# A state-space block: u by one Silu pass of ScalarE in place of tanh, copy and a VectorE multiply; step projection and skip products moved

## What is computed

```
xz = in_proj_w @ xn                       # 512 rows: x (256) and z (256)
for each direction (the second on reversed tokens):
    u = silu(causal_conv(x, conv_w) + conv_b)          # 256 x 512, four taps
    x_dbl = xproj_w @ u                                # 8 + 16 + 16 rows: steps, B, C
    delta = softplus(dtproj_w @ x_dbl[:8] + dt_bias)   # 256 x 512
    h[l] = exp(delta * A) * h[l-1] + delta * B * u     # 256 channels x 16 states
    y = (h * C).sum(states) + D * u
    out += y * silu(z)
result = x + out_proj_w @ out + quantised_linear(hadamard(xn))
```

## Time and profile before

| | |
|---|---|
| median of 3 runs | 977.38 us (975.98 to 980.18) |
| profiled execution | 976.08 us, span 974.0 us |
| TensorE busy | 765.9 us, 79% (3873 matmuls) |
| VectorE busy | 800.2 us, 82% |
| ScalarE busy | 782.1 us, 80% |
| GpSimd busy | 750.2 us, 77% |
| mean granted TensorE clock | 0.864 of full speed |
| DMA | 72.53 MB, mean 74 GB/s |

### The profile page before, as it was taken

How to read it: one execution, slowest core, us unless ns; L and a number is a source line. 1 busy time by engine, 2 the same in 40 slices (tenths; PEclk the granted TensorE clock), 3 DMA queues, 4 the chain that set the end, 5 groups by cost and what they waited for, 6 DMA issues and landing times.

```text
span 974.0 us, 13835 instructions
## 1 busy us (share of the span) xinstructions
PE 765.9 (79%) x3873; PEld 384.4 (39%) x3873; DVE 800.2 (82%) x838; ACT 782.1 (80%) x1454; POOL 750.2 (77%) x454
## 2 busy tenths in 40 slices
PE   3486977689786977979689697878978697797994
PEld 1233443343433435334353344434443343433452
DVE  2278988898788878888888887889878887897995
ACT  2599995899878987789967998589986898878970
POOL 2159887788768977789787887878886798777994
PEclk9788988889787988979889797988978798897797
DMA  3424225070620607024070512507052070702400
GB/s 91 113 66 118 48 79 107 4 163 4 141 55 30 135 3 172 24 70 91 30 166 3 126 38 70 124 3 162 3 126 68 10 154 3 172 14 68 95 7 27
DMA packets 51433, 72.53 MB, mean 74 GB/s; under 512 B 6704, under 2 KB 19920, under 8 KB 51408
## 3 DMA queue, kind: packets, MB, share of 16 engines
q1 hardware_dynamic: 50976, 71.97, 31.6%
q10 hardware_dynamic: 432, 0.26, 0.1%
HBM read 60.68 MB, written 11.53 MB: 74 GB/s over the span
## 4 chain that ended last, share of the span: by engine, by line
POOL 29%; issue 27%; PE 18%; ACT 15%; DVE 8%; DMA 2%; POOLq 1%; SPq 0%; DVEq 0%; ACTq 0%
POOL hst L678 22%; PE pb L792 5%; DVE hst L569 5%; ACT da L416 4%; POOL dbx_t L688 4%; PE b_ps L879 4%; ACT dbx_t L405 2%; PE y L894 2%; PE b_ps L864 1%; PE y L891 1%; POOL t_log L694 1%; ACT xn L308 1%; PE pb L856 1%; DVE b_ps L557 1%; PE pb L811 1%
## 5 line engine op out<-in xcount | busy, mean ns | idle before, releaser
L678 POOL TENSOR_TENSOR hst<-hst,c_rep 128x1024 f32<-128x1024 f32 x256 | 600.6, 2365 | 170.8 <-DVE hst L569 170.1
L569 DVE TENSOR_TENSOR_SCAN hst<-da,b_ps 128x512 f32<-128x512 f32 x512 | 586.3, 1202 | 43.1 <-ACT da L416 21.4
L879 PE MATMUL b_ps<-ident,dbx_t 128*128 128x128 f32 x1536 | 246.6, 301 | 158.3 <-DVE hst L569 157.4
L416 ACT ACTIVATE da<-rep,neg_a 128x511 f32<-128x511 f32 x512 | 336.2, 710 | 5.8 <-DVE hst L569 3.8
L879 PEld LDWEIGHTS b_ps<-ident,dbx_t 128*128 128x128 f32 x1536 | 181.0, 151 | 281.2 <-DVE hst L569 255.7
L405 ACT ACTIVATE dbx_t<-du_t,b_t 128x256 f32<-128x256 f32 x576 | 247.0, 496 | 2.5 <-PE b_ps L879 1.7
L894 PE MATMUL y<-hst,sum_sel 128*32 128x512 f32 x1024 | 148.9, 657 | 3.0 <-POOL hst L678 3.0
L792 PE MATMUL pb<-xnt,conv_wt 128*128 128x512 f32 x256 | 121.0, 617 | 0.8 <-ACT xnt L316 0.8
L688 POOL TENSOR_TENSOR dbx_t<-du_t,b_t 128x1024 f32<-128x1024 f32 x48 | 91.3, 1903 | 2.7 <-ACT du_t L388 2.7
L864 PE MATMUL b_ps<-t_log,spread_sel 32*128 32x512 f32 x256 | 73.4, 679 | 14.3 <-POOL t_log L740 9.8
L557 DVE TENSOR_TENSOR b_ps<-b_ps,b_rep 128x1024 f32<-128x1024 f32 x64 | 78.0, 1219 | 5.4 <-PE b_ps L864 5.4
(11 more groups left out here) (111 smaller groups left out, 588.5 us busy)
## 6 DMA issues: line engine op xcount, KB each, us to landing
rep<-d_scr SPq DMA_DIRECT2D x128, 256.0 KB, 9.1
c_rep<-bc_scr SPq DMA_DIRECT2D x64, 256.0 KB, 4.8
d_scr<-t_pos SPq DMA_DIRECT2D x15, 512.0 KB, 3.0
b_rep<-bc_scr SPq DMA_DIRECT2D x64, 64.0 KB, 2.2
x_ln<-x SPq DMA_DIRECT2D x8, 256.0 KB, 3.3
x_res<-x SPq DMA_DIRECT2D x8, 256.0 KB, 2.8
out<-x_res SPq DMA_DIRECT2D x8, 256.0 KB, 7.1
conv_wt<-conv_w SPq DMA_DIRECT2D x2, 512.0 KB, 5.8
```

The lines of the kernel that those rows point to most:

```text
L416: nc.scalar.activation(da[s % 2][:, j, 1:L], rep[d][h][:, j, 1:L], ACT.Exp, scale=neg_a[:, d, h, j, q:q + 1]).then_inc(decay_done, 1)
L569: nc.vector.tensor_tensor_scan(hst[s % RING][:, j, :], da[s % 2][:, j, :], b_ps[:, j, :], 0.0, ALU.mult, ALU.add).then_inc(scan_done, 1)
L678: nc.gpsimd.tensor_tensor(hst[s % RING][:, two, :], hst[s % RING][:, two, :], c_rep[d][:, q:q + 1, :].broadcast_to([P, 2, L]), ALU.mult).t ...
L879: ins = tr(b_ps[:, j, P * c:P * (c + 1)], dbx_t[(NX * d + q - 1) % 2][:, c, NJ * h + j, :, :].rearrange("p r e -> p (r e)"), ident[:, :])
```

## The change

u becomes one ScalarE activation with function Silu, reading the convolution's bank with the bias and writing u. Both halves follow each other at the end of slot 0, and VectorE has no u operation left. `half_bias` goes with it. keep_bt moves ahead of slot 2's second pair of decays. The projection weight is there once, x_dbl once (64 partitions), and two weight loads (four DMAs) fewer are issued. On TensorE `steps` for h = 1 moves to right behind `b_transposed`, between the two halves of slot 2's inputs; the skip products move from the sums to slot 3, between the two halves of slot 4's inputs (`SKIP_AT` is 3). Some waits change to match.

```diff
-        xproj = [sb(f"xproj{d}", [P, NH, 2, XC]) for d in range(2)]
+        xproj = [sb(f"xproj{d}", [P, NH, XC]) for d in range(2)]
...
-                for h in range(NH):
-                    sp.dma_start(xproj[d][:, :, h, 0:DR + 2 * NS], xproj_t[d]).then_inc(w_loaded, DMA)
-                    sp.dma_start(dtw[d][XC * h:XC * h + DR, :], dt_t[d]).then_inc(w_loaded, DMA)
+                sp.dma_start(xproj[d][:, :, 0:DR + 2 * NS], xproj_t[d]).then_inc(w_loaded, DMA)
+                sp.dma_start(dtw[d][0:DR, :], dt_t[d]).then_inc(w_loaded, DMA)
...
-            def u_sigmoid(d, V, h):
+            def make_u(d, V, h):
                 act.wait_ge(conv_filled, 2 * V + h + 1)
-                wait(act, delta_ready, V)
-                nc.scalar.activation(t_exp[:, h, :], pb[:, 1 - h, :], ACT.Tanh, bias=half_bias[:, d, h:h + 1], scale=0.5).then_inc(u_step, 1)
-                act.wait_ge(u_step, 2 * V + h + 1)
-                nc.scalar.activation(t_exp[:, h, :], t_exp[:, h, :], ACT.Copy, bias=0.5, scale=0.5).then_inc(u_sig, 1)
+                if h == 0:
+                    wait(act, sum_done, SLOTS * (V - 2) + SKIP_AT)
+                    wait(act, du_ready, V - 1)
+                nc.scalar.activation(u[d][:, h, :], pb[:, 1 - h, :], ACT.Silu, bias=col[:, d, 0, h:h + 1]).then_inc(u_ready, 1)
 
             def keep_xdbl(d, V):
...
-                nc.scalar.activation(xdbl[d][:, :], pb[:, 1, :], ACT.Copy).then_inc(xdbl_ready, 1)
+                nc.scalar.activation(xdbl[d][0:XC, :], pb[0:XC, 1, :], ACT.Copy).then_inc(xdbl_ready, 1)
...
             def softplus_in(d, V):
-                wait(act, u_ready, 2 * V + 2)
+                wait(act, delta_ready, V)
...
-                        if nxt:
-                            u_sigmoid(e, V, 1)
                     if s == 2:
                         if nxt:
                             keep_xdbl(e, V)
                         if d == 0 and not first(b):
                             keep_xqt(b - 1)
                         inputs_t(d, U, 2, 2)
+                        if nxt:
+                            keep_bt(e, V)
...
                     if s == 0:
                         inputs_t(d, U, 1, 2)
                         if nxt:
-                            u_sigmoid(e, V, 0)
+                            make_u(e, V, 0)
+                            make_u(e, V, 1)
...
                         if nxt:
-                            keep_bt(e, V)
                             softplus_in(e, V)
...
-            def make_u(d, V, h):
-                dve.wait_ge(u_sig, 2 * V + h + 1)
-                wait(dve, sum_done, SLOTS * (V - 2) + SKIP_AT)
-                nc.vector.scalar_tensor_tensor(u[d][:, h, :], pb[:, 1 - h, :], col[:, d, 0, h:h + 1], t_exp[:, h, :], ALU.add, ALU.mult).then_inc(u_ready, 1)
...
-                    ins = mm(pb[:, 1, :], xproj[d][:, h, :, :].rearrange("p r c -> p (r c)"), u[d][:, h, :], start=h == 0, stop=h == NH - 1)
+                    ins = mm(pb[0:XC, 1, :], xproj[d][:, h, :], u[d][:, h, :], start=h == 0, stop=h == NH - 1)
...
-                mm(pb[:, h, :], dtw[d][XC * h:XC * (h + 1), P * h:P * (h + 1)], xdbl[d][XC * h:XC * (h + 1), :], start=True, stop=True).then_inc(dt_filled, 1)
+                mm(pb[:, h, :], dtw[d][0:XC, P * h:P * (h + 1)], xdbl[d][0:XC, :], start=True, stop=True).then_inc(dt_filled, 1)
...
+            def skip_products(b, d):
+                step = slice(None, None, -1 if d else 1)
+                pe.wait_ge(u_ready, 2 * (2 * b + d) + 2)
+                for h in range(NH):
+                    mm(y[:, h, :], skip[:, d, h, :], u[d][:, h, step], start=False, stop=False, skip_group_check=True)
+
             def sum_states(b, d, s):
...
-                if s == SKIP_AT - 1:
-                    pe.wait_ge(u_ready, 2 * (2 * b + d) + 2)
-                    for n in range(NH):
-                        mm(y[:, n, :], skip[:, d, n, :], u[d][:, n, step], start=False, stop=False, skip_group_check=True)
...
                             b_transposed(e, V, u_ready, 2 * V + 2)
+                        steps(e, 1, xdbl_ready, V + 1)
+                    if s == SKIP_AT:
+                        skip_products(b, d)
...
                     if s == 1 and nxt:
-                        steps(e, 1, xdbl_ready, V + 1)
                         steps(e, 0, bt_ready, V + 1)
```

More of the change, by code:

```diff
@@ L50, in build @@
         col = sb("col", [P, 2, 3, NH])
-        half_bias = sb("half_bias", [P, 2, NH])
-        xproj = [sb(f"xproj{d}", [P, NH, 2, XC]) for d in range(2)]
+        xproj = [sb(f"xproj{d}", [P, NH, XC]) for d in range(2)]
         dtw = [sb(f"dtw{d}", [P, DI]) for d in range(2)]
@@ L137, in build @@
         conv_filled = sem("conv_filled")
-        u_step = sem("u_step")
-        u_sig = sem("u_sig")
         u_ready = sem("u_ready")
@@ L282, in _ @@
             sp.wait_ge(out_stored, DMA * NB)
-        W_LOADS = 7 + 8
+        W_LOADS = 7 + 4
         WIN = hst[0][:, 0, 0:DI]
@@ L354, in first_softplus @@
             def first_softplus():
-                act.wait_ge(u_ready, 2)
                 act.wait_ge(dt_filled, 1)
@@ L423, in _ @@
             nc.scalar.activation(neg_a[:, :, :, :, :], neg_a[:, :, :, :, :], ACT.Exp).then_inc(a_exp, 1)
-            act.wait_ge(weights_ready, 3)
-            u_sigmoid(0, 0, 0)
-            u_sigmoid(0, 0, 1)
+            make_u(0, 0, 0)
+            make_u(0, 0, 1)
             keep_xdbl(0, 0)
@@ L588, in _ @@
             dve.wait_ge(w_loaded, DMA * W_LOADS)
-            nc.vector.tensor_scalar(half_bias[:, :, :], col[:, :, 0, :], 0.5, None, ALU.mult).then_inc(weights_ready, 1)
             for d in range(2):
@@ L607, in _ @@
             nc.vector.tensor_scalar(neg_a[:, :, :, :, :], neg_a[:, :, :, :, :], -1.0, None, ALU.mult).then_inc(weights_ready, 1)
-            make_u(0, 0, 0)
-            make_u(0, 0, 1)
             dve.wait_ge(fwt_filled, 1)
@@ L631, in unit @@
                     scan(b, d, s, 0)
-                    if s == 0 and nxt:
-                        make_u(e, V, 0)
                     if s == 1 and d == 0 and not first(b):
@@ L646, in unit @@
                     scan(b, d, s, 1)
[L647 to L651, removed]
+                    if s == 0 and d == 0 and not first(b):
+                        gate_y(b - 1, 0)
                     if s == 1 and d == 0 and not last(b):
@@ L907, in _ @@
             pe.wait_ge(w_loaded, DMA * W_LOADS)
-            pe.wait_ge(weights_ready, 5)
+            pe.wait_ge(weights_ready, 4)
             x_proj(0, 0)
```

## The result

The changed kernel takes 1028.13 us as a median (1027.81 to 1030.9, 4 runs) against 978.26 us before: a ratio of 1.0517 (1.0486 to 1.0548), 50 us slower. I had forecast slower, but 992 us, and the range ended at 1008. The profiled execution took 1027.81 us with a span of 1026.0.

What follows compares the result with a forecast made beforehand. No engine is full; a chain that changes engines bounds the kernel. Unit d = 1 seven times 1.9 us (13.3), unit d = 0 eight times 0.5 (4), less 1: 976 + 16 = 992 us, range 969 to 1008.

Steps and rivals of the forecast that it cites:

- My 3.16 us for the decays of slot 1: First half of unit d = 1: both Silu passes and a table load start slot 1's second decays 3.16 us later.
- for Tanh I had 1.76: Without table loads beside Silu, as Tanh needs none beside Exp, the decays move by 1.76 us, not 3.16.
- the moved steps' term: Step projections behind xdbl, now apart: 0 to 2.2 us late depending on TensorE's clock, taken as 0.5 us.
- Unit d = 1: First half, where ScalarE never rests over 1.4 us: later decays and steps cost 2.3 us (1.8 to 4.0).
- Unit d = 0: First half: the softplus' old wait for steps takes up ScalarE's delay; late steps cost 0 to 2.2 us, taken as 0.5.
- a wait of 3.14 us would absorb the 3.15: First half of unit d = 0: ScalarE moves 3.15 us, but softplus waited 3.14 for steps, so it arrives at 416.19, not 416.18.
- my third rival: Clock stays low behind each wait for xdbl and the moved steps are the bound: 1024 us, 8%.
- 0.9 us for the convolution: Second half: if the clock falls longer in TensorE's grown gap before scan (6,1), the convolution loses 0 to 0.9 us, taken as 0.2.
- The skip products: Moved into the gap ahead of slot 4's inputs, they free slot 5's scan and the residual in unit d = 1: 0.6 us mean gain.
- the bound: GpSimd's scales become the next late thing before VectorE's reciprocal, so 0.9 of the 2.7 us can be kept.
- unit d = 0's second half: The gain at slot 5 ends at GpSimd's refine, for which ScalarE's normalisation waits: 0.
- Setup and first units: Setup costs 0, its Silu load hidden before the first convolution; 1 us off for the first unit, partly covered by a DMA wait.

## Why the prediction was wrong

**The direction and its cause were right.** 66 loads instead of 34, two round each pair of Silu passes. My 3.16 us for the decays of slot 1 measured 3.18; for Tanh I had 1.76 and the run shows 7.88 - 6.14 = 1.74. A Silu ends at 483.64, the load starts at 483.66 and the decay at 484.95. The drain of 1380 ns beside each load, which the Trainium skill states (page "ScalarE: Activation LUTs", section "What ACT_TABLE_LOAD costs"), has no room there.

**The step that failed is the moved steps' term.** I had TensorE's row behind xdbl between full and half clock, 0 to 2.2 us late, and took 0.5 in every unit, with no row for that choice between the two. Measured, the clock was 0.50 to 0.52 over the whole row in all 15 units, and the row is longer than I had it even at half clock, since b_transposed too doubles (1.88 for 1.06). Unit d = 1 costs, over convolution, xdbl and softplus, 3.18 + 0.82 = 4.0 us, or 4.7 beside those units before whose steps ran at full clock (24.62 against 19.94 from the second pass to log1p); I had 2.3, so the steps' term is 2.2 us as a mean, the top of my bounds. Unit d = 0 costs 3.18 - 0.16 = 3.0; I had 0.5, and 2.2 at most. Together that is 7 x 1.7 + 8 x 2.5 = 32 of the 36 us between 992 and 1028. In unit d = 0 the reading that a wait of 3.14 us would absorb the 3.15 was the error: that wait was in part TensorE's own slow row, and the row came again, slower, behind the later xdbl. This is my third rival, which I gave 8% and 1024 us. It had unit d = 1 right (4.0 us) and unit d = 0 too low (2.2); that its number came within 4 us owes something to luck, since it also counted 0.9 us for the convolution.

**The skip products.** The reciprocal comes 0.57 us earlier after log1p, against 0.6 forecast, and VectorE's wait for GpSimd's scales rose from 3.2 us in 2 batches to 13.9 in 8, as the bound said. What I had at no cost was unit d = 0's second half: 0.84 us are lost there to the clock, and are gone with the skip products taken back, which makes the changed kernel 5 us faster.

**Setup and first units.** I had nothing but 1 us to take off; 8.9 us had come by the second log1p (V = 2), 2.7 of them by the first. There the row from xdbl to softplus is 9.61 us instead of 7.17, the same half clock.

**What I said would show it.** Two loads a unit, a 1.85 us idle before the second Silu, the second decays 3.75 us after that Silu's end, Abs waiting for TensorE at a low clock, the reciprocal waiting for GpSimd: seen. VectorE's wait for Ln longer than 2.7 us: wrong, it is at most 2.0, since VectorE now waits ahead of it for slot inputs that the same slow row delays. The wait at the residual is not gone but shorter, 7.4 us in 8 places after 16.6.

**What stays open** is how much of the difference between the two versions with Silu in slot 1 is the skip products' clock: the one with them taken back varied by 20 us from execution to execution. With the skip products in slot 3, u on ScalarE is worse than tanh, copy and multiply even in slot 1, 981.0 against 965.6 us with no overlap of the executions. With them in their old place it was not shown to be better or worse: 968 against 961 us, with overlapping ranges. And which of the moves gave the 16 us was not tested.

## What to carry to other kernels

Put an operation with a wait behind the independent work of its engine, not ahead of it: the same two passes and the same loads cost 62 us at the end of slot 0 and 15 us half a slot later, against a kernel with the same moves and u made the old way. Where a move lengthens a wait of TensorE inside a chain, price the whole row behind that wait at half clock too, small matmuls included, and not only the one instruction that was moved. And test parts of a change alone, since here one part gained 16 us and was buried under another.

## What the runs showed of the hardware

Twice the clock made a change of order act against its intent. Idle time of 3.35 us was followed by 9.7 us at 0.50, so that a row of instructions took twice as long as at full clock; and 2.7 us of useless matmuls in that gap kept the clock at full for the whole row in four of seven units, for part of it in the others, and made the kernel 13 us faster. The wait's length alone does not tell the clock: with Silu in slot 1 it was 0.56 behind a wait of 0.93 us. Filling a gap with useful work (the skip products) did not remove the half clock but moved it some 15 us on, from instructions that nobody waited for to ones on the chain.
